# Handing over gathers and freeing ring slots two groups at a time

## What is computed

```python
# each of the three graph convolutions
agg = jax.ops.segment_sum(x[src], dst, num_segments=N)
h = agg @ W_rel + b + x @ W_root
# batch-norm layer: the edges have weights
msgs = edge_vals[:, None] * x[edge_src]
agg = jax.ops.segment_sum(msgs, edge_dst, num_segments=N)
```

## Time and profile before

| | us |
|---|---|
| median of 3 runs | 8811.06 |
| lowest and highest run | 8798.18, 8813.36 |
| profiled execution | 8823.46 |
| its span, first to last instruction | 8822.0 |

### The profile page before, as it was taken

How to read it: one execution, slowest core, us unless ns; L and a number is a source line. 1 busy time by engine, 2 the same in 40 slices (tenths; PEclk the granted TensorE clock), 3 DMA queues, 4 the chain that set the end, 5 groups by cost and what they waited for, 6 DMA issues and landing times. The chain is left out here.

```text
span 8822.0 us, 84511 instructions
## 1 busy us (share of the span) xinstructions
PE 4974.4 (56%) x17588; PEld 3810.7 (43%) x17589; DVE 3959.5 (45%) x6997; ACT 877.5 (10%) x2210; POOL 5531.9 (63%) x5865
## 2 busy tenths in 40 slices
PE   0355555355554466676666665666656667355554
PEld 0234444244443344555444554455544545244443
DVE  2466666466667322233222342222622226466667
ACT  0000001200002000011000020000333333100000
POOL 2477771477772577755777657776377770577770
PEclk6677777777776677787778887788777788777777
DMA  2344442544442333333333333333433332544442
GB/s 97 109 118 116 118 117 62 151 118 117 117 117 74 112 105 105 105 104 104 105 105 105 103 106 105 105 105 103 122 105 105 105 105 87 157 119 118 118 119 71
DMA packets 465797, 956.30 MB, mean 108 GB/s; under 512 B 118628, under 2 KB 269288, under 8 KB 464879
## 3 DMA queue, kind: packets, MB, share of 16 engines
q0 software_dynamic: 277216, 753.12, 31.1%
q1 hardware_dynamic: 172795, 193.39, 7.2%
q10 hardware_dynamic: 15552, 7.59, 0.3%
HBM read 875.47 MB, written 84.60 MB: 109 GB/s over the span
## 5 line engine op out<-in xcount | busy, mean ns | idle before, releaser
L1359 POOL DMA_INDIRECT l1aa_messages<-table,l1aa_index x784 | 743.4, 948 | 294.6 <-issue 238.7
L1359 POOL DMA_INDIRECT l2a_messages<-table,l2a_index x784 | 743.5, 948 | 277.9 <-issue 238.7
L1359 POOL DMA_INDIRECT l1ca_messages<-table,l1ca_index x784 | 743.6, 948 | 248.7 <-issue 238.7
L1359 POOL DMA_INDIRECT l1ba_messages<-table,l1ba_index x784 | 743.3, 948 | 248.6 <-issue 238.7
L1472 PE MATMUL l1aa_sums<-l1aa_messages,l1aa_member 128*128 x1952 | 608.3, 482 | 511.0 <-SPq L1368 501.5
L997 POOL DMA_INDIRECT l0ba_messages<-table_h,l0ba_index x782 | 746.7, 955 | 238.5 <-issue 238.1
L997 POOL DMA_INDIRECT l3a_messages<-table_h,l3a_index x782 | 746.3, 954 | 238.4 <-issue 236.9
L997 POOL DMA_INDIRECT l0aa_messages<-table_h,l0aa_index x782 | 746.0, 954 | 238.4 <-issue 238.4
L1472 PE MATMUL l2a_sums<-l2a_messages,l2a_member 128*128 x1952 | 610.6, 483 | 419.0 <-ACT l2a_messages L1407 412.7
L1472 PE MATMUL l1ca_sums<-l1ca_messages,l1ca_member 128*128 x1952 | 606.8, 481 | 395.6 <-SPq L1368 390.1
L1472 PE MATMUL l1ba_sums<-l1ba_messages,l1ba_member 128*128 x1952 | 603.9, 479 | 398.2 <-SPq L1368 390.9
(11 more groups left out here) (685 smaller groups left out, 6784.6 us busy)
## 6 DMA issues: line engine op xcount, KB each, us to landing
l2b_xin<-table SPq DMA_DIRECT2D x100, 128.0 KB, 2.1
l1aa_messages<-table,l1aa_index POOLq DMA_INDIRECT x784, 2.8
l1ba_messages<-table,l1ba_index POOLq DMA_INDIRECT x784, 2.8
l1ca_messages<-table,l1ca_index POOLq DMA_INDIRECT x784, 2.8
l2a_messages<-table,l2a_index POOLq DMA_INDIRECT x784, 2.8
l0aa_messages<-table_h,l0aa_index POOLq DMA_INDIRECT x782, 2.8
l0ba_messages<-table_h,l0ba_index POOLq DMA_INDIRECT x782, 2.8
l3a_messages<-table_h,l3a_index POOLq DMA_INDIRECT x782, 2.8
```

The lines of the kernel that those rows point to most:

```text
L1359: pool.indirect_dma_start(out=ring4[:, g % ROUND, j, 0:D], out_offset=None, in_=table, in_offset=bass.IndirectOffsetOnAxis(ap=index[:, g * ...
```

## The change

The relay and the free now work on pairs of groups, g and g+1 with g even.

- `relay` waits for the semaphores of both slots and then adds 2 to `ready`.
- `free` waits until the second group of the pair has been read, and adds 2 to `slot_free`. One table entry is loaded for a pair, that of g+1.
- GpSimd waits before even groups only, for the pair to which its slot belongs.
- SyncE's order is relay of the pair g+2, free of the pair g; the loop has five rounds of eight pairs.

ScalarE, VectorE and TensorE have the same instructions as before. In the weighted pass the frees alone change, since SyncE has no relays there. The table's counts are the same.

```diff
             for g in range(NGROUP):
-                if g >= ROUND:
-                    pool.wait_ge(slot_free, g - ROUND + 1)
+                if g >= ROUND and g % 2 == 0:
+                    pool.wait_ge(slot_free, g - ROUND + 2)
...
-            def relay(i, s):
-                sp.wait_ge(gathered[s], i * (16 * U) + 16 * U)
-                sp.sem_inc(ready, 1)
-
-            def free(i, s):
-                g = i * ROUND + s
-                needed = nc.values_load(steps.frees[0:1, bass.ds(g, 1)], engines=(mybir.EngineType.SP,),
+            def relay(g, i):
+
+                for s in (g % ROUND, g % ROUND + 1):
+                    sp.wait_ge(gathered[s], i * (16 * U) + (g // ROUND + 1) * (16 * U))
+                sp.sem_inc(ready, 2)
+
+            def free(g, i):
+
+                needed = nc.values_load(steps.frees[0:1, bass.ds(i * ROUND + (g + 1), 1)], engines=(mybir.EngineType.SP,),
                                         min_val=0, max_val=QSTEP, skip_runtime_bounds_check_because="made so")
                 wait_table(sp, step_summed, needed)
-                sp.sem_inc(slot_free, 1)
+                sp.sem_inc(slot_free, 2)
...
             else:
-                for s in range(LEAD):
-                    relay(0, s)
+                relay(0, 0)
             with sp.Fori(0, rounds - 1) as i:
-                for s in range(ROUND):
+                for g in range(0, ROUND, 2):
                     if not weighted:
-                        relay(*later(i, s, LEAD))
-                    free(i, s)
-            for n in range(rest):
-                if not weighted:
-                    relay(*later(rounds - 1, n, LEAD))
-                free(rounds - 1, n)
+                        relay(g + 2, i)
+                    free(g, i)
             if not weighted:
-                for n in range(rest, ROUND + rest - LEAD):
-                    relay(*later(rounds - 1, n, LEAD))
+                relay(2, rounds - 1)
+            free(0, rounds - 1)
+            if not weighted:
+                for g in range(4, ROUND + rest, 2):
+                    relay(g, rounds - 1)
```

## The result

The kernel before takes 8808.43 us (median of 11 runs, 8798.18 to 8813.36), the changed kernel 8833.97 us (11 runs, 8830.78 to 8838.97): 25.5 us slower, ratio 1.003 with a 95% interval of 1.0020 to 1.0039. The forecast was 30.1 us slower, 8841.2 us, in a range from 8823 to 8857. The sign, the place and the mechanism hold. The size came out 15% smaller; the interval, 18 to 34 us, holds the forecast too, so it is the trace that tells the two apart. And the end of a pass has something in it that the prediction denied.

A forecast was written before the change was run, and what follows sets the result against it. GpSimd's gathers were taken to bound the kernel. Three convolution-pass tails of 10.04 us plus zero for all other terms gave 30.1 us, on the median of 8811.06 us making 8841.2 us, range 8823 to 8857.

The forecast's parts named there:

- the bound and the place: GpSimd's gathers, 1.253 us each, bound all four passes; TensorE's lateness costs time only behind a pass's last gather.
- the zeros: Second relay wait on SyncE, frees in pairs, 164 GpSimd waits removed, end of the weighted pass: 0 us each.
- one sign of the prediction: GpSimd's gather spacing stays at 1.253 us; if shorter, the waits had a price (a rival, chance 0.05).
- the shape of the tail: Each convolution pass ends with one run of 48 matmul records, starting 4.3 us after the last gather's start.
- the length of the last run: End of each convolution pass: three units take 13.76 us where one took 3.72, costing 10.04 us a pass.
- the thirteen runs: 48-record runs in the earlier kernel's convolution passes, 13.57 to 13.83 us; the 13.76 us one, after 6.36 us idle, was taken.
- The range from single units: Last run with a first unit of 5.14 to 6.75 us: 12.58 to 14.19 us, three tails 26.6 to 31.4 us.
- nothing else lies between: At a pass's end, only the last add precedes the next phase's first transfer, so a later last unit moves everything.
- tail hidden: Rival, chance 0.07: something else, such as a later barrier, starts the next phase, so a later last unit costs nothing; 8811 us.
- The fall of TensorE's time: TensorE's matmul time in a pass falls from 608 to about 563 us, with at most 49 relay waits; gains nothing.

The follow-up runs named there:

- experiment 1: The changed kernel with only the last pair's relay, groups 96 and 97, made single again: 8804.36 against 8803.89 us for the kernel before, ratio 1.0001.
- experiment 2: Two kernels, each the kernel before with one part changed: first, relays in pairs only, 8825.51 us, ratio 1.0025; second, frees in pairs only, 8804.19 us, ratio 1.0001.

## Why the prediction was right, and where it wasn't

**Right: the bound and the place.** That lateness of TensorE counts only behind the last gather is shown by experiment 1, which undoes one relay of 49 and gets everything back.

**Right: the zeros.** Frees in pairs, 164 waits less, the second relay wait of a pair, and the weighted pass. The second kernel of experiment 2 shows the first two (ratio 1.0001), experiment 1 the third, with 48 relays in pairs (1.0001). `l2a` has its last add at +12.37 (+12.42 before), and its first transfer at +13.68 (+13.73). By one sign of the prediction the waits had a price: the gathers' spacing fell, from 1.2531 to 1.2516 us. It is no effect of the waits. With all 82 waits (relays in pairs only) it is 1.2501 us, with 41 (frees in pairs only) 1.2499, and what moved is the length of a gather (948 to 947 ns), not the gap (238.7 to 238.6 us in all).

**Right: the shape of the tail.** One run of 48 records that starts 4.1 to 4.5 us behind the last gather's start, 4.3 was forecast.

**Mis-sized: the length of the last run**, forecast at 13.76 us, measured at 13.51, 13.00 and 13.44, worth 1.3 us in the sum. The step that failed is to take a row with a similar idle time before it, since the length doesn't go by that. The changed kernel has 69 runs of 48 records in its three passes, 12.03 to 13.66 us long, among them these two, one behind the other:

```profile
3695.81 13.53 PE L1470 MATMUL l1aa_sums<-l1aa_messages,l1aa_member 128*128 x48 [10.17 <-SPq L1371]
3715.80 12.08 PE L1470 MATMUL l1aa_sums<-l1aa_messages,l1aa_member 128*128 x48 [6.47 <-SPq L1371]
```

And the thirteen runs that the prediction chose from are the long ones by selection. In the kernel before, a third unit joins a run only if the first two still go on when the next group comes, 10.02 us later; shorter ones stand there as runs of 32 records (7.19 to 10.14 us). This is argued from the rows, not shown by an experiment. The range from single units, 12.58 to 14.19 us, holds the three last runs, but not the 12.35 us of the kernel with relays in pairs only, and also has a step that failed: it took 3.72 us for units B and C, the length of a unit by itself, where the adds behind them come 3.46 us apart (3903.95, 3907.41, 3910.87 in `l1aa`). With 3.46 the range is 12.06 to 13.67 us, which is nearly what the 69 runs show.

**Wrong: "nothing else lies between".** The prediction took the last add for what ends a pass, because it was the last record of work. GpSimd's drain ended 1 us later and set the end. So the first microsecond by which the tail grew was free: 1.89 - 0.89 = 1.00, 2.13 - 0.87 = 1.26, 1.87 - 0.86 = 1.01, together 3.3 us. The "tail hidden" rival was true for 3.3 of 28.5 us. The rows had a number that should have been asked about, the 1.9 us from the last add to the next transfer, where 0.9 are enough in the changed kernel; the prediction used it as evidence that nothing was in between. In the sum: 30.1, less 1.3 for the runs, less 0.25 for their earlier start, less 3.3 for the drain, is 25.3 us.

**The fall of TensorE's time** was forecast at 608 to 563 us and came to 545. The 49 first units were sized right: those of the changed kernel's 138 runs of 32 and 48 records average 5.9 to 6.0 us, forecast 5.95. Too long were again the others, at 3.72 instead of 3.46 us: 49 x 5.95 + 73 x 3.46 = 544 us.

## What to carry to other kernels

A consumer that keeps up with its producer pays for the size of a portion once, at the end, with everything that arrives in the last portion; so make portions single at the end. In the middle they may be coarse, but here that gave nothing back either (experiment 1). Before a tail is priced, look at what the barrier behind it waited for, on every engine and drains included: work that looks last may have cover, and the first microseconds of a longer tail are then free. And a mechanism that is hidden by another engine's bound can be the bound on another chip, so a time is to be compared with the kernel before on the same chip only.

## What I had not expected of the hardware

- **GpSimd's drain.** The drain at the end of a block with indirect gathers takes 24.0 to 24.3 us in the traces at the usual speed, begins before the last gathers have started, and ends 10.0 to 10.2 us behind the start of the last one, though this one has landed and been relayed at about +4.3. Its end goes with the last gather and not with its own length: in five traces at the other speed it takes 15.9 to 21.9 us, and ends 9.9 to 10.3 us behind that start in all their twenty passes (as 4781.7 + 15.9 against 4787.4, 4774.7 + 21.8 against 4786.3). What it waits for, the traces don't say.
- **The last gather lands late.** Its relay lets TensorE start 4.1 to 4.6 us behind its start, where groups with further gathers behind them took 3.0 (3894.56 - 3891.57). SyncE's wait for it lasted 11.4 us in `l1aa` of the kernel before, 1.4 more than a group's 10.02, and ended on the transfer. The late start is there wherever, at the usual speed, TensorE stood waiting for the last gather.
- **Gathers differ from execution to execution.** They take 945 to 948 ns in the mean of one, and the kernel doesn't decide which: 948 and 946 in the two profiles of the version with 782 gathers. With the gap it is 1.2503 us a gather in the second of these, 1.2532 in that of the kernel without the last unit on the same chip, 1.2531 before and 1.2516 after the change. Over the 5500 gathers of a run, 0.003 us are 16 us, which is about the spread of the runs (8798 to 8813).
- **Chips on which this kernel takes 22 to 23% longer.** GpSimd's, VectorE's and ScalarE's instructions last as long there as elsewhere (a gather 945 to 948 ns), and so do TensorE's (379 and 380 ns in the median), but in the passes over edges it gets matmuls one by one. After the last gather they come densely again, 247 records in 55.79 us. Why is open.
